# Expert-choice selection: a threshold search with three bits a round in place of two, its tests split between VectorE and ScalarE

## The reference

```python
scores = (x_flat @ Wg.T).T                                # 8 x 4096
top_vals, token_idx = jax.lax.top_k(scores, capacity)     # the best 512 of 4096
token_w = jax.nn.softmax(top_vals, axis=-1)
xg = x_flat[token_idx]
h = silu(einsum(xg, W1)) * einsum(xg, W3)
y = einsum(h, W2) * token_w[..., None]
out = zeros_like(x_flat).at[token_idx.reshape(-1)].add(y.reshape(-1, c))
```

## Time and profile before

| | us |
|---|---|
| median of 3 runs | 817.49 |
| lowest and highest | 813.66, 818.08 |
| span of the profiled execution | 814.1 |
| TensorE, VectorE, ScalarE, GpSimd busy | 690.2, 632.6, 486.0, 313.7 |

### The profile page before, as it was taken

One profiled execution on the slowest core, in us unless ns is written; L12 is line 12 of the kernel. 1 busy time (PEld: TensorE's weight loads), 2 busy tenths in 40 slices (PEclk: granted clock), 3 DMA queues, 4 the chain that ended last, 5 costly groups with the idle time before them and its releaser, 6 DMA issues.

```text
span 814.1 us, 11786 instructions
## 1 busy us (share of the span) xinstructions
PE 690.2 (85%) x4152; PEld 529.5 (65%) x4152; DVE 632.6 (78%) x1244; ACT 486.0 (60%) x621; POOL 313.7 (39%) x249
## 2 busy tenths in 40 slices
PE   6882029999999888999999999999999999009998
PEld 5761026899888754566566656577887888007998
DVE  5988894887777388887767675987888899997654
ACT  2223012554454437796896886666655999796873
POOL 4353604377677735234422420003440444693000
PEclk9995558999999999999999999999999999658999
DMA  9927523456644570010013000003310743201343
GB/s 299 339 81 257 200 80 110 127 137 146 178 88 58 108 254 1 1 47 27 1 47 130 1 27 27 27 27 133 127 52 1 261 152 131 76 0 53 125 135 104
DMA packets 59540, 84.95 MB, mean 104 GB/s; under 512 B 7904, under 2 KB 47712, under 8 KB 57952
## 3 DMA queue, kind: packets, MB, share of 16 engines
q1 hardware_dynamic: 49936, 61.09, 22.3%
q0 software_dynamic: 7872, 21.11, 10.5%
q10 hardware_dynamic: 1680, 2.08, 0.8%
HBM read 53.73 MB, written 30.54 MB: 104 GB/s over the span
## 4 chain that ended last, share of the span: by engine, by line
PE 63%; DVE 14%; ACT 7%; issue 4%; POOL 3%; DMA 1%; POOLq 0%; DVEq 0%; ACTq 0%
PE bank L2101 13%; PE bank L2363 11%; PE bank L2157 8%; PE bank L2387 5%; PE bank L1448 3%; PE bank L1482 3%; PE bank L1505 3%; PE bank L1542 3%; PE bank L1502 3%; DVE above L783 2%; PE bank L1463 2%; PE bank L1486 2%; ACT wgateT L2050 1%; DVE qx L1179 1%; ACT qT L1331 1%
## 5 line engine op out<-in xcount | busy, mean ns | idle before, releaser
L1305 ACT ACTIVATE x<-bank,bic 128x512 f32<-128x512 f32 x160 | 106.2, 697 | 34.1 <-PE bank L1482 32.6
L1179 DVE TENSOR_REDUCE qx<-bank 128x4 fp32r<-128x616 f32 x128 | 98.2, 796 | 27.0 <-PE bank L1448 25.6
L2101 PE MATMUL bank<-ux,uwh 128*128 128x512 f32 x384 | 96.6, 393 | 0.2 <-ACT ux L1995 0.2
L2101 PEld LDWEIGHTS bank<-ux,uwh 128*128 128x128 f32 x384 | 72.5, 189 | 16.0 <-issue 0.6
L1482 PE MATMUL bank<-qT,K 128*128 128x512 f32 x128 | 61.5, 490 | 3.5 <-ACT x L1305 2.0
L2324 ACT ACTIVATE wgateT<-bank 128x512 f32<-128x512 f32 x32 | 19.2, 599 | 65.7 <-PE bank L2363 65.7
L1448 PE MATMUL bank<-Kb,qTb 128*128 128x308 bf16 x256 | 53.2, 298 | 4.9 <-DVE qx L1179 2.2
L2101 PE MATMUL bank<-ux,uwl 128*128 128x512 f32 x192 | 52.0, 393 | 0.0
L1106 POOL CAST qx<-q 128x1024 fp32r<-128x1024 f32 x8 | 8.5, 1068 | 112.7 <-PE bank L1463 104.0
L2363 PE MATMUL bank<-xh,wh 128*128 128x512 f32 x128 | 50.0, 390 | 0.3 <-DVE xl L2297 0.3
L2363 PE MATMUL bank<-xl,wh 128*128 128x512 f32 x128 | 50.0, 390 | 0.0
(11 more groups left out here) (420 smaller groups left out, 2029.0 us busy)
## 6 DMA issues: line engine op xcount, KB each, us to landing
xs_dram<-ux POOLq DMA_DIRECT2D x6, 1024.0 KB, 4.2
ux<-xs_dram POOLq DMA_DIRECT2D x6, 1024.0 KB, 5.3
x_dram<-x SPq DMA_DIRECT2D x4, 1024.0 KB, 5.5
xr<-in_w1T SPq DMA_DIRECT2D x8, 512.0 KB, 3.8
xr<-in_w3T SPq DMA_DIRECT2D x8, 512.0 KB, 4.7
xr<-in_w2T SPq DMA_DIRECT2D x8, 512.0 KB, 6.5
row_dram<-xn SPq DMA_DIRECT2D x8, 512.0 KB, 3.1
x_dram<-xr SPq DMA_DIRECT2D x8, 512.0 KB, 2.9
```

The lines of the kernel that those rows point to most:

```text
L1179: dve.tensor_reduce(qx[:, k, g * GH:(g + 1) * GH, MROW].rearrange("p (u h) -> p u h", u=2), pair[i][:].rearrange("p (u x) -> p u x", u=2)[ ...
L1305: act.activation(pr[g % 2][h], S_[u % 2], ACT.Exp, bias=bic[:, s // 2, h // GH:h // GH + 1]).then_inc(p_done, 1)
L2101: mm = pe.matmul(bank[j][:, m * TB:(m + 1) * TB], w[:, c * HI + cols:c * HI + cols + P], x[:, part, c * TB:(c + 1) * TB], start=(w is uwh ...
```

## The change

A round finds three bits, with seven thresholds. There are ten such rounds and the last one with a single threshold (3 x 10 + 1 = 31 bits as 2 x 15 + 1). HIGH becomes 8. The first four thresholds are tested by VectorE as before. The other three are tested by ScalarE: it computes Sign(threshold - `odd`), where `odd` is `v` with its lowest bit set, so that the difference is never zero, and its accumulator sums the signs of a partition. TensorE multiplies these sums by `neg16`, which is -0.5 where `blk16` is 1, into columns 4 to 6 of the same bank; the result is the count less N/2, and `wants` has N/2 less in these columns. The comparison becomes a scalar_tensor_tensor with a tile of wanted counts. ScalarE loads the table of Sign first, then does its part of the ten rounds, and only behind them the exponentials and the three casts. One unused semaphore of a later stage is left out (not shown).

```diff
@@ -32,7 +32,9 @@
 HEADS, HD = 16, 16
 HI = 768
 HIC = HI // P
-DIGITS = 15
+DIGITS = 10
+TESTS = 7
+SIGNS = 3
 QB = 32
 EPS = 1e-5
 STEP = 4
...
@@ -51,7 +53,7 @@
 C_ID, C_ONE, C_BLK, C_TRI = 0, P, 2 * P, 3 * P
 C_IND = 4 * P
 C_END = C_IND + E
-G_TOKEN = 3 * DIGITS + 1
+G_TOKEN = TESTS * DIGITS + 1
 G_PLACE = G_TOKEN + 2 * P
 G_END = G_PLACE + P
 
...
@@ -66,7 +68,7 @@
     c[:, C_TRI:C_TRI + P] = same & (pair[:, None] < pair[None, :])
     c[:, C_IND:C_IND + E] = expert[:, None] == np.arange(E)
     c[:, C_ONE:C_ONE + P] = 1.0
-    digit = (np.arange(1, 4) << (29 - 2 * np.arange(DIGITS)[:, None])).reshape(-1)
+    digit = (np.arange(1, TESTS + 1) << (28 - 3 * np.arange(DIGITS)[:, None])).reshape(-1)
     grid = np.zeros((P, G_END), np.float32)
     grid[:, 0:G_TOKEN] = np.append(digit, 1)
     grid[:, G_TOKEN:G_PLACE] = (2 * pair + np.arange(2)[:, None]).reshape(-1) * P + p[:, None] - N // 2
...
@@ -308,7 +310,7 @@
         sg = sb(l0, "sg", [P, 2 * P])
         shift = sb(l0, "shift", [P, NT])
         grid = sb(l0, "grid", [P, G_END])
-        blk16, tri16 = sb(l0, "blk16", [P, P], BF16), sb(l0, "tri16", [P, P], BF16)
+        blk16, tri16, neg16 = (sb(l0, n, [P, P], BF16) for n in ("blk16", "tri16", "neg16"))
         x1_out = sem("x1_out")
         RING = 4
         rows_in = [sem(f"rows_in{i}") for i in range(RING)]
...
@@ -614,6 +616,7 @@
                     pool.wait_ge(cst_in, 48)
                     pool.tensor_copy(blk16[:], cst[:, C_BLK:C_BLK + P])
                     pool.tensor_copy(tri16[:], cst[:, C_TRI:C_TRI + P])
+                    pool.tensor_scalar(neg16[:], cst[:, C_BLK:C_BLK + P], -0.5, 1.0, ALU.mult, ALU.mult)
 
                 @block.tensor
                 def _(pe):
...
@@ -714,12 +717,15 @@
 
 
         with ExitStack() as st:
-            above = [sb(st, f"above{j}", [P, 2 * P]) for j in range(3)]
-            cand, tail = sb(st, "cand", [P, 3], I32), sb(st, "tail", [P, 3], I32)
-            base = sb(st, "base", [P, 2, 3])
+            LEVELS = TESTS - SIGNS
+            above = [sb(st, f"above{j}", [P, 2 * P]) for j in range(LEVELS)]
+            signs = [sb(st, f"signs{j}", [P, 2 * P], BF16) for j in range(SIGNS)]
+            odd = sb(st, "odd", [P, 2 * P])
+            cand, tail = sb(st, "cand", [P, TESTS], I32), sb(st, "tail", [P, TESTS], I32)
+            base = sb(st, "base", [P, 2, TESTS])
             thr = sb(st, "thr", [P, 1], I32)
-            cnt3, cnt0 = sb(st, "cnt3", [P, 3], BF16), sb(st, "cnt0", [P, 1], BF16)
-            got = sb(st, "got", [P, 3])
+            cnt4, cnt0, sgn3 = sb(st, "cnt4", [P, LEVELS], BF16), sb(st, "cnt0", [P, 1], BF16), sb(st, "sgn3", [P, SIGNS], BF16)
+            got, wants = sb(st, "got", [P, TESTS]), sb(st, "wants", [P, TESTS])
             v, ex = sb(st, "v", [P, 2 * P]), sb(st, "ex", [P, 2 * P])
             junk = sb(st, "junk", [P, 2 * P])
             gt, eq, cgt, ceq = (sb(st, n, [P, 2 * P]) for n in ("gt", "eq", "cgt", "ceq"))
...
@@ -737,12 +743,15 @@
             hot_id = sb(st, "hot_id", [P, CELLS, 16, 4], F16)
             wT = sb(st, "wT", [P, NT, E])
             ids = sb(st, "ids", [P, 2, 16, 4])
-            half, want, cnt, rowmax, negmax, star, need, sume, rsum, bits, gone, before = (small[:, i:i + 1] for i in range(12))
+            half, spare, cnt, rowmax, negmax, star, need, sume, rsum, bits, gone, before = (small[:, i:i + 1] for i in range(12))
             d_dve, d_cnt, d_pe, d_act, d_out = (sem(n) for n in ("d_dve", "d_cnt", "d_pe", "d_act", "d_out"))
-            d_tot, d_mid, d_row, d_sum, d_hot, d_place = (sem("d_" + n) for n in "tot mid row sum hot place".split())
+            d_tot, d_mid, d_row, d_sum, d_hot, d_place, d_sgn = (sem("d_" + n) for n in "tot mid row sum hot place sgn".split())
             d_put = [sem(f"d_put{i}") for i in range(2)]
-            UNIT = [float(1 << max(29 - 2 * n, 0)) for n in range(DIGITS + 1)]
-            HIGH = 12
+            UNIT = [float(1 << max(28 - 3 * n, 0)) for n in range(DIGITS + 1)]
+            HIGH = 8
+            ROUND_AT = [2]
+            for n in range(DIGITS - 1):
+                ROUND_AT.append(ROUND_AT[-1] + (2 if n < HIGH - 1 else 4 if n == HIGH - 1 else 3))
             onesw = ones[:, 0:1].broadcast_to([P, 2 * P])
             TOK = bank[3][:, 512:512 + P].rearrange("p (q l e) -> p q l e", q=2, e=4)
             MAXES, MAXROW, PRIOR, SLOTS, EXPS, WTS, IDS, SPREAD, GATHERED = range(1, 10)
...
@@ -772,20 +781,24 @@
                 dve.wait_ge(d_pe, 1)
                 ch.link(dve.tensor_scalar(half, bank[1][:, 0:1], CAP - 0.5, 0.5, ALU.is_ge, ALU.subtract))
                 ch.step(dve.tensor_scalar(v[:], sg[:], half, 2.0, ALU.mult, ALU.mult))
-                ch.step(dve.tensor_scalar(want, half, float(2 * CAP - N - 1), 0.5 * (N + 1), ALU.mult, ALU.add))
-                tot.step(dve.tensor_copy(cand[:], grid[:, 0:3]))
+                tot.step(dve.tensor_copy(cand[:], grid[:, 0:TESTS]))
+                ch.wait()
+                tot.step(dve.tensor_scalar(odd[:].bitcast(I32), v[:].bitcast(I32), 1, None, ALU.bitwise_or))
+                for cols, less in ((slice(0, LEVELS), 0), (slice(LEVELS, TESTS), N // 2)):
+                    ch.step(dve.tensor_scalar(wants[:, cols], half.broadcast_to([P, cols.stop - cols.start]), float(2 * CAP - N - 1),
+                                              0.5 * (N + 1) - less, ALU.mult, ALU.add))
                 ch.step(dve.memset(found[:], 0.0))
                 ch.wait()
 
                 def tested(n, tests):
                     tot.wait()
-                    for j in range(tests):
+                    for j in range(min(tests, LEVELS)):
                         dve.tensor_scalar(above[j][:], v[:], cand[:, j:j + 1].bitcast(F32), 0.0, ALU.is_ge, ALU.add,
-                                          accum_out=cnt3[:, j:j + 1]).then_inc(d_cnt, 1)
+                                          accum_out=cnt4[:, j:j + 1]).then_inc(d_cnt, 1)
 
                 def counted(n, tests):
                     dve.wait_ge(d_pe, n + 2)
-                    tot.link(dve.tensor_scalar(got[:, 0:tests], bank[1][:, 0:tests], want, 0.0, ALU.is_ge, ALU.add, accum_out=cnt))
+                    tot.link(dve.scalar_tensor_tensor(got[:, 0:tests], bank[1][:, 0:tests], 1.0, wants[:, 0:tests], ALU.mult, ALU.is_ge, accum_out=cnt))
 
                 def maxima(n):
                     if n == 1:
...
@@ -798,22 +811,22 @@
                                                  ALU.mult, ALU.mult, accum_out=negmax).then_inc(d_mid, 1)
 
                 for n in range(DIGITS + 1):
-                    tests = 3 if n < DIGITS else 1
+                    tests = TESTS if n < DIGITS else 1
                     now, nxt = found[:, n % 2:n % 2 + 1], found[:, (n + 1) % 2:(n + 1) % 2 + 1]
-                    wide = 3 if n + 1 < DIGITS else 1
-                    steps = grid[:, 3 * n + 3:3 * n + 3 + wide] if n < DIGITS else None
+                    wide = TESTS if n + 1 < DIGITS else 1
+                    steps = grid[:, TESTS * (n + 1):TESTS * (n + 1) + wide] if n < DIGITS else None
                     tested(n, tests)
                     if n < DIGITS and n != HIGH - 1:
                         ch.link(dve.tensor_scalar(base[:, n % 2, 0:wide], steps, now, None, ALU.add))
                     maxima(n)
                     counted(n, tests)
                     if n < HIGH - 1:
-                        tot.step(dve.scalar_tensor_tensor(cand[:], cnt.broadcast_to([P, 3]), UNIT[n], base[:, n % 2, :], ALU.mult, ALU.add))
+                        tot.step(dve.scalar_tensor_tensor(cand[:], cnt.broadcast_to([P, TESTS]), UNIT[n], base[:, n % 2, :], ALU.mult, ALU.add))
                         ch.link(dve.scalar_tensor_tensor(nxt, cnt, UNIT[n], now, ALU.mult, ALU.add))
                     elif n == HIGH - 1:
                         tot.step(dve.scalar_tensor_tensor(thr[:], cnt, UNIT[n], now, ALU.mult, ALU.add))
                         tot.link(dve.tensor_copy(tail[:], steps))
-                        tot.step(dve.tensor_tensor(cand[:], tail[:], thr[:].broadcast_to([P, 3]), ALU.bitwise_or))
+                        tot.step(dve.tensor_tensor(cand[:], tail[:], thr[:].broadcast_to([P, TESTS]), ALU.bitwise_or))
                         ch.link(dve.memset(nxt, 0.0))
                     elif n < DIGITS:
                         tot.link(dve.scalar_tensor_tensor(tail[:, 0:wide], cnt.broadcast_to([P, wide]), UNIT[n], base[:, n % 2, 0:wide],
...
@@ -873,6 +886,13 @@
                     weights_lo(m)
 
             def search_scalar(act):
+                act.preload_act_table(ACT.Sign)
+                for n in range(DIGITS):
+                    act.wait_ge(d_tot, ROUND_AT[n])
+                    for j in range(SIGNS):
+                        with nc.allow_low_precision(reason="even sums up to 256 are exact in 16 bits"):
+                            act.activation(signs[j][:], odd[:], ACT.Sign, bias=cand[:, LEVELS + j:LEVELS + j + 1].bitcast(F32), scale=-1.0,
```

(13 more changed lines are left out.)

## The result

The changed kernel takes 809.34 us (median of 7 runs, 807.73 to 810.66) against 817.49 (7 runs, 813.36 to 819.43): a ratio of 0.991, with a 95% interval of 0.989 to 0.993 (the ratio is taken over all the runs; the two medians alone give 0.990). By the medians that is 8.15 us less where 6.9 were forecast (810.6). The span of the profiled execution fell from 814.1 to 805.9.

What follows compares the result with a forecast made beforehand. VectorE's serial threshold search was taken to bound its stage. Search 7.4 us shorter, less 0.5 before the loop, gives 6.9: span 814.1 to 807.2, plus 3.4 outside it, makes 810.6 us; range 807 to 815.

Steps and rivals of the forecast that it cites:

- The bound: Threshold search: a serial loop of sixteen rounds on VectorE, 35.46 us, with nothing else under way that the end waits for.
- rival A: Search rounds: VectorE sets the round and ScalarE's sign tests stay hidden behind it; 810.6 us, chance 0.76.
- B: Search rounds: ScalarE sets the round mildly, at 0.70 us a sign test; gain 4.1 us, time 813.4, chance 0.12.
- C: Search rounds: ScalarE sets the round outright, a sign test at three times VectorE's 0.40 us; 829.2 us, chance 0.04.
- D: Behind the search: search shortens but the end stays, something with its own schedule ending last; 817.5 us, chance 0.06.
- A further test at 0.40 us: VectorE in a search round: each threshold test beyond the present three adds 0.40 us, making the quiet high-bit round 2.60.
- A sign test at 0.52 us: ScalarE in a search round: 0.52 us per sign test, three ending after 1.65 us, hidden behind VectorE by 0.12.
- The non-overlapping 0.70: ScalarE's sign test if its two instructions did not overlap: 0.70 us each, ten rounds losing 2.8 us.
- The time by that rule, 829: Skill's rule against ScalarE elementwise work: a sign test of 1.2 us, ScalarE setting the round, about 829 us.
- Product against comparison: Search rounds: TensorE's second product adds 0.5 us in all, the shorter comparison gives back 0.5; taken to cancel.
- Before the loop: Ahead of the search: the "odd" pass, 0.35 us, and two "wants" plus a wait, some 0.15; 0.5 us added.
- the disturbance: Search's high-bit rounds: 1.22 us over the quiet rounds, partly GpSimd stretching VectorE, partly reading maxima; 1.0 kept after the change.

Runs made afterwards that it cites:

- e1: Changed kernel with three tests on VectorE and four on ScalarE instead of four and three; 812.08 us, ratio 0.9953 to the kernel before.
- e2: Changed kernel with five tests on VectorE and two on ScalarE instead of four and three; 813.35 us, ratio 0.9976 to the kernel before.
- e3: Changed kernel with all seven tests on VectorE, no signs, "odd" copy or second product; 820.43 us, ratio 1.0071 to the kernel before.
- e6: Kernel before with GpSimd's row normalisation held until the search ends; search 33.80 us against 35.46, whole kernel 846.94 us, one run.
- e7: Changed kernel with GpSimd's row normalisation held until the search ends; search 26.26 us against 26.90, whole kernel 836.85 us, one run.
- e11: Changed kernel unaltered, run again for a second profile; search 27.20 us against 26.90, whole kernel 811.41 us, one run.
- e12: Kernel before unaltered, run again for a second profile; search 34.67 us against 35.46, whole kernel 813.97 us, one run.
- e4: Changed kernel put back to fifteen two-bit rounds, two tests on VectorE and one on ScalarE; 810.41 us, ratio 0.9943 to the kernel before.

## Why the prediction was right

**The bound** (rival A) held: VectorE's tests set the round, ScalarE is hidden, and nothing behind the search took the gain back. Rivals B and C fall with the rows of the round and with e1, which is what they look like when made to happen. D falls with the runs' medians, 8.15 us apart where it has none, and with the gather, which moved by 8.1 us in the first pair of profiles and 6.9 in the second.

**A further test at 0.40 us**: right; the group of four takes 1.70 on the chain, e2's search is 4.0 us longer for one more test in ten rounds, and e3 is 0.1 us from what three more make.

**A sign test at 0.52 us**: 0.51 for the first, 0.49 for the others, so the three take 1.59 us, not 1.65. ScalarE's margin is 0.19 us a round and not 0.12: the 0.24 above, less the 0.05 that e1 has between the last sum and the product. The non-overlapping 0.70 was too pessimistic a bound: accumulator and pointer bias together cost no more than apart. The page "ScalarE: Activation LUTs" of the Trainium skill, section "Rules for kernel authors", would have kept such work off ScalarE, with VectorE "up to about 3×" faster in bf16. This trace, in fp32, has a test at 1.2 times VectorE's price (0.49 against 0.40 us), and on an engine that was idle beside the path, which the rule doesn't weigh. The time by that rule, 829, didn't come.

**Product against comparison**: forecast to cancel. The products are 0.05 apart and the comparison 0.17 long, as forecast, but the step from the first product's start to that of "cand" fell from 0.58 to 0.53, since the second product overlaps the first and ends only 0.03 later, while the comparison gives back more than that. That is why the quiet round is 2.56, not 2.60.

**Before the loop**: 0.43 us more than before (1.96 from the stage's first operation to the first test, against 1.53), forecast 0.5.

**The mis-sized term is the disturbance.** The sum took the round between the kinds at 3.25, from a disturbed 2.85, and kept 1.0 in the seven high-bit rounds. Measured, the high-bit rounds are 17.99 us in place of 19.2, the round between 2.87 in place of 3.25, the low ones 6.04 in place of 5.60: 1.15 us less in all. Quiet against quiet (e6, e7) the change is worth 33.80 - 26.26 = 7.54 us in the search, less 0.28 ahead of it (1.80 against 1.52 there, "odd" being unstretched): 7.3, close to the 6.9 of the sum. The rest of the first profiles' 8.1 is that 1.66 us of stretches met the one and 0.64 the other, and by e11 and e12 (0.87 and 0.94) that is chance. The measured 8.15 has an interval of about 5.7 to 9.0, which holds both. So the mechanism and its price are shown, and that the measured gain came out above the forecast is not more than luck.

## What to carry to other kernels

Price a serial search by what a bit costs: (fixed part of the round + tests on the busiest engine) / bits. More bits a round lost on one engine and won on two; the split of the tests was worth more than the bits. Count the cover behind a step in dependent operations, at the length they have when disturbed: 0.32 us of TensorE's time hid two small ones only while both were quiet, and the second one, moved there to save 0.09, cost more than it saved. And when a term is read from rows that differ between like rounds, find out first whether the difference belongs to the round or to a neighbour, because the next execution deals it anew.

## What the hardware showed that was not expected

GpSimd's passes stretch VectorE's short operations from 0.15 to 0.23 up to 0.57 us ("base" in e3, "cand" in e4) and the pass "odd" of 128x256 from 0.29 to 0.46, and never the tests of 128x256 with an accumulator (473 to 481 ns with GpSimd and without) or the comparison that reads PSUM (at most 0.22 throughout). The other way round, a GpSimd pass of 0.54 us beside the tests takes 19.42/16 = 1.21 us in e6, where it meets VectorE's ranking and one-hot operations. "SBUF — State Buffer" of the Trainium skill, section "SBUF: two separate sides", describes a port pair that GpSimd shares with those VectorE operations that read two inputs from SBUF or run in a two-port mode, held for a whole instruction. That fits what was stretched (cand reads two tiles of SBUF, the tests one) and what wasn't. "odd" reads one tile and a constant, so of the two conditions only the mode is left for it; the trace doesn't show modes, and which of the two caught "base", with one tile and one pointer, no run here shows.
